# The first heads' values of each pass laid between the parts of the first cross attention

## The chip, the cores and the metric

One NeuronCore of a Trainium2 chip runs the whole program. The metric is the time of one execution on the device in microseconds (us); the kernel before took 2357.95 us, the median of 3 runs (2356.15 to 2360.07). Engines: TensorE (PE, matrix products), VectorE (DVE), ScalarE (ACT), GpSimd (POOL), and SyncE (SP), which here only issues DMAs.

## What is computed

Two layers on x and ctx, both 8 batches of 256 rows of 512, all in float32. The first is a small attention without softmax, with 1x1 convolutions over the 256 rows; the second has two multi-head cross attentions (16 heads of 128) with the same ctx, and an MLP.

```
g_x = conv(g_w, g_b, ctx)^T ; theta_x = conv(theta_w, theta_b, x)^T ; phi_x = conv(phi_w, phi_b, ctx)
W = theta_x @ phi_x / 512 ; y = (W @ g_x)^T
x = batch_norm(conv(w_w, w_b, y)) + x
for l in (1, 2):
    h = layer_norm(x) * scale_l + offset_l
    q, k, v = h @ wq_l + bq_l, ctx @ wk_l + bk_l, ctx @ wv_l + bv_l
    k, v = (k, v with one bias row more, for each head)
    x = x + (softmax(q @ k^T / sqrt(128)) @ v) @ wo_l + bo_l
x = x + gelu((layer_norm(x) * scale + offset) @ w_fc1 + b_fc1) @ w_fc2 + b_fc2
```

## The kernel before

**Precision.** A product of two float32 matrices is made of three fp32r products: each operand is split into a high part (rounded) and a low part (the rest), and `product` (lines 781 to 783) adds high x high, high x low and low x high. So whatever PE multiplies has first been split: weights by POOL, the context and the results by ACT (high) and DVE (low).

**The front part.** Keys and values of both cross attentions depend on ctx alone and are made first and stored in HBM (`kd`, `vd`). The 2048 rows of ctx are taken in two passes of 1024 (`PAIRS`). A pass has eight rounds (`GROUPS`), so rounds r = 0 to 15; a round makes the keys and values of four heads for the pass's 1024 rows. Keys are made by a scheme of seven products in place of eight (`K`, r, i, k: head pair i = 0, 1; P1, P6, P2, P7, P5, P3, P4), from sums of blocks of the weights (`sums`, `keys` on POOL, lines 601 to 640) and sums of blocks of the turned context (T1 to T4, made in `blocks`). Such a group of seven takes 42 instructions on PE. Values are plain: eight row tiles (`V`, r, t) of 12 instructions. A round is K(r, 0), K(r, 1), then V(r, 0) to V(r, 7). A finished key block (`C`) or value tile is staged by ACT and DVE in one of four slots of `stage` and sent by SP.

**The opening.** Ahead of rounds 0 and 8 stands `opening(p)` (line 109): the first cross attention for the four batches b of the pass, in the parts `pg` (two products of ctx with phi and g weights), `M` (their product, 128x128), `th` (theta), `WM`, and `wy` (twice; then ACT makes `aff`, DVE adds x to it, which counts `z_x`, 16 in all, 8 for a pass). Its results pass through PSUM banks S, T and O; ACT copies M, th and WM (`msb`, `th`, `wm`), and DVE adds the bias of pg. Between these parts stand the transposes of the context for the key scheme (`B`, p, i, blk: four blocks for each i), through the four banks of U. In pass 0 ACT and DVE also make the high and low parts of the plain context from the same banks (lines 1036, 1272); the sums T1 to T4 go to a buffer `temp(i, form)`, ACT makes their high part (1044) and POOL the low one (`forms_lo`, 589).

**What sets the order.** Nothing is scheduled: each engine walks the same list `FRONT`, written by `front_order()` and `opening(p)`, in order, and does its part of every item. Only POOL has an order of its own (lines 717 to 745). Semaphores name the counts that an item waits for. PE's wait for an item's weights is on `k_form` (seven for a group of keys) or `split_v` (one for each half of a round's value weights).

```
for r in range(ROUNDS):
    if r % GROUPS == 0:
        for i in range(2):
            forms_lo(r // GROUPS, i)
        sums(r, 1)
        values(r, 0)
        values(r, 1)
        keys(r, 1)
    else:
        values(r, 0)
        keys(r, 1)
        values(r, 1)
    value_bias(r)
```

Behind this, for every round, come `sums(r + 1, 0)` and `keys(r + 1, 0)`, and `sums(r + 1, 1)` where r + 1 isn't the first round of a pass. `keys(r, i)` is seven casts and seven subtractions into `wks`, each cast waiting until PE has used the former form of the same number.

**Buffers.** Many lie over each other. Raw value weights of rounds 0 and 8 (`early_v`) lay over `stage`, as did both early buffers of key sums (`early_s`); later rounds use `rawv` and `ks`, over `pg` and `xb` of the first cross attention. `temp` lay in `z` and in the region `spare`, over `tmp`, `vb` and `raw_vb`.

Of the kernel before, what the change touches and what calls it, by code (L numbers as in the profile page):

```python
# [37 lines left out]
P = 128  # L38
# [70 lines left out]
def opening(p):  # L109

    def blocks(i):
        return [("B", p, i, blk) for blk in range(4)]

    b = 4 * p
    out = [("pg", b, 0), ("pg", b, 1)] + blocks(0)
    for b in range(4 * p, 4 * p + 4):
        more = b + 1 < 4 * p + 4
        out += [("M", b, 0)] + ([("pg", b + 1, 0)] if more else [])
        out += [("th", b, 0), ("WM", b, 0)] + ([("pg", b + 1, 1)] if more else [])
        out += blocks(1) if b == 4 * p else []  # L120
        out += [("wy", b, 0), ("wy", b, 1)]
    return out


def front_order():

    out = []
    for r in range(ROUNDS):
# [112 lines left out]
def bass_xattn(nc, x_in, ctx_in, thw, thb, pgw, pgb, www, bncol, wa, wk, wv, wb, hcol, vrow,  # L241
               lncol, f1col, orow, out):
    ctx = ExitStack()
    with ctx:
# [32 lines left out]
        (wks,) = at(r, 16384, ("wks", [2, 7, 2, P], F32R))  # L277
        wqs, wos = at(r, 16384, ("wqs", [2, CH, 256], F32R), ("wos", [2, 2, D], F32R))
# [6 lines left out]
        early_v = at(r, 8192, ("early_v0", [CH, 256], F32), ("early_v1", [CH, 256], F32))  # L285
        early_s = at(r + 8256, 8256, ("early_s0", [4, 2, P], F32)) + at(r + 3 * 4128, 4128, ("early_s1", [4, 2, P], F32))
# [12 lines left out]
        z = sb("z", [4, D])  # L299
# [4 lines left out]
        (ts,) = at(r, 10240, ("ts", [4, 512], F32))  # L304
# [85 lines left out]
        def temp(i, form):  # L390
            return z[:, form, :] if i == 0 else ts[:, form, :]
# [23 lines left out]
        def _(sp):  # L415
# [17 lines left out]
            def load_value_weights(r):  # L433

                e = r % GROUPS
                for i in range(2):
                    if r:
                        sp.wait_ge(split_v[i], r)
                    if r == GROUPS:
                        for k in range(4):  # L440
                            sp.wait_ge(sent[k], 16 * len(KV) // 8)
# [5 lines left out]
                if e == 0:  # L447
                    sp.wait_ge(t_lo, 8 * (r // GROUPS + 1))
# [3 lines left out]
            def load_x(b):  # L452

                if b == 5:
                    sp.wait_ge(k_form, 7 * (quad(GROUPS, 0) + 1))
# [32 lines left out]
            load_x(0)  # L488
            load_key_weights(0, 0)
            load_x(1)  # L490
            load_key_weights(0, 1)
            bias_row(0)
            load_x(2)
            load_chunk(2)
            load_value_weights(0)
            load_chunk(3)
            load_x(3)

            for what, *a in FRONT:
                if what == "C":  # L500
# [5 lines left out]
                    if (i, o) == (0, C11):  # L506
                        if r + 1 < ROUNDS:
# [8 lines left out]
                elif what == "V":  # L516
# [6 lines left out]
                    if t == 1 and (r + 1) % GROUPS:  # L523
# [3 lines left out]
                    if r == GROUPS - 1 and t == PAIR_TILES - 1:  # L527
                        load_value_weights(GROUPS)
                        load_x(6)
                        load_x(7)  # L530
                    if t == 2 and r + 1 == ROUNDS:
# [5 lines left out]
                        load_values(0)  # L537
            for i in range(4):
# [29 lines left out]
        def _(pool):  # L568
# [975 lines left out]
```

## Time and profile before

| | before |
|---|---|
| median of 3 runs | 2357.95 us |
| the profiled execution | 2355.32 us, its span 2353.5 us |
| PE busy | 2308.7 us (98%) |
| DVE, ACT, POOL busy | 1488.8, 1177.4, 892.9 us |
| chain that ended last | PE 87%, ACT 5%, DVE 3%, POOL 2%, issue 2% |
| granted PE clock, whole span | 0.997 |
| first opening, keys of round 0, values of round 0 | 9.12 to 60.2, to 79.3, to 101.1 us |
| second opening | 390.5 to 430 us |

The span is the time from the first to the last instruction. Matmul records overlap, since the array is pipelined: in a dense stretch a 128x512 fp32r product starts every 0.227 us though its record is 0.39 us long. For the length of a step, starts are to be compared, not durations. The granted clock is a share of 2.4 GHz.

### The profile page before, as it was taken

The page shows a single profiled execution, that of the slowest core. Times are in us where ns is not written, and L with a number is a line of the kernel's source. Part 1 is how long each engine was busy: PE and PEld are TensorE (multiplying, and loading weights), DVE is VectorE, ACT ScalarE, POOL GpSimd, SP SyncE. Part 2 cuts the span into 40 slices and gives each one's busy share as a digit, 9 for nine tenths or more (in the row PEclk, how much of TensorE's full clock was granted, in tenths as well). Part 3 has the DMA queues.
Part 4 walks back from the last instruction along what each step waited for, and adds up shares of the span by engine and source line. Part 5 has one row for each costly group of instructions (what it writes and reads, how often), then busy time and mean ns, then how long its engine had stood idle before and what let it go on. Part 6 is the DMA issues. An engine that isn't in the chain of part 4 may idle for free.

```text
span 2353.5 us, 33519 instructions
## 1 busy us (share of the span) xinstructions
PE 2308.7 (98%) x12144; PEld 1961.7 (83%) x12144; DVE 1488.8 (63%) x2444; ACT 1177.4 (50%) x2897; POOL 892.9 (38%) x876
## 2 busy tenths in 40 slices
PE   7999999999999999999999999999999998999999
PEld 4888888788887788888888878888888887788887
DVE  4777767777777666666666776666666666534433
ACT  3322224322323866666666677666666667322222
POOL 5787876688786430011100253211101114611110
PEclk9999999999999999999999999999999999999999
DMA  4677775577777433333334323343334330100001
GB/s 169 233 269 271 266 278 198 197 251 280 268 267 252 159 121 134 131 126 123 138 121 141 126 85 124 133 141 125 117 126 143 128 134 29 34 30 27 28 1 72
DMA packets 147937, 352.88 MB, mean 150 GB/s; under 512 B 9536, under 2 KB 75584, under 8 KB 131392
## 3 DMA queue, kind: packets, MB, share of 16 engines
q1 hardware_dynamic: 147056, 350.65, 42.9%
q8 instruction: 99, 1.62, 0.3%
q14 instruction: 62, 0.51, 0.1%
q10 hardware_dynamic: 720, 0.10, 0.0%
HBM read 211.78 MB, written 138.94 MB: 149 GB/s over the span
## 4 chain that ended last, share of the span: by engine, by line
PE 87%; ACT 5%; DVE 3%; issue 2%; POOL 2%; DMA 0%; SPq 0%; DVEq 0%; ACTq 0%; POOLq 0%
PE U L781 22%; PE U L783 22%; PE U L782 22%; PE T L909 4%; PE O L781 2%; PE O L783 2%; PE S L783 2%; PE O L782 2%; PE S L781 2%; PE S L782 2%; ACT probs L1125 1%; ACT aff L1084 1%; POOL z L705 1%; ACT probs L1117 1%; DVE hT L1358 1%
## 5 line engine op out<-in xcount | busy, mean ns | idle before, releaser
L580 POOL CAST wos<-raw 128x1024 fp32r<-128x1024 f32 x20 | 20.9, 1047 | 852.9 <-PE U L783 852.9
L1377 DVE TENSOR_TENSOR x<-x,U 128x512 f32<-128x512 f32 x384 | 261.2, 683 | 80.8 <-PE U L783 78.6
L1385 DVE TENSOR_REDUCE nm<-S 128x2 f32<-128x514 f32 x256 | 177.3, 693 | 123.4 <-PE S L783 119.6
L1117 ACT ACTIVATE probs<-S,nm 128x257 f32<-128x257 f32 x512 | 237.7, 476 | 27.2 <-DVE nm L1385 27.2
L1135 ACT ACTIVATE PT<-T 128x512 fp32r<-128x512 f32 x256 | 152.5, 596 | 173.3 <-PE T L909 172.8
L1125 ACT ACTIVATE probs<-probs,rs 128x256 f32<-128x256 f32 x512 | 230.1, 500 | 0.5 <-DVE rs L1389 0.5
L1400 DVE SCALAR_TENSOR_TENSOR oT<-O,hc,oT 128x256 fp32r<-128x256 f32 x256 | 123.8, 484 | 143.1 <-ACT oT L1144 143.1
L781 PE MATMUL U<-wos,oT 128*128 128x512 f32 x512 | 213.4, 417 | 0.3 <-DVE gT L1368 0.2
L1072 ACT ACTIVATE stage<-tmp 128x512 fp32r<-128x512 f32 x128 | 81.1, 633 | 243.9 <-DVE tmp L1350 235.5
L783 PE MATMUL U<-wos,oT 128*128 128x512 f32 x512 | 202.0, 395 | 0.0
L1393 DVE TENSOR_TENSOR PT<-T,PT 128x512 fp32r<-128x512 f32 x256 | 175.5, 686 | 41.8 <-ACT PT L1135 41.8
L782 PE MATMUL U<-wos,oT 128*128 128x512 f32 x512 | 201.3, 393 | 0.0
L781 PE MATMUL U<-wvs,plain 128*128 128x512 f32 x512 | 201.0, 393 | 0.0
L783 PE MATMUL U<-wvs,plain 128*128 128x512 f32 x512 | 200.0, 391 | 0.0
L782 PE MATMUL U<-wvs,plain 128*128 128x512 f32 x512 | 199.9, 390 | 0.0
L1144 ACT ACTIVATE oT<-O,hc 128x256 fp32r<-128x256 f32 x256 | 121.2, 473 | 126.3 <-PE O L783 126.3
L1066 ACT ACTIVATE stage<-z 128x512 fp32r<-128x512 f32 x128 | 81.0, 633 | 196.2 <-DVE z L1311 195.7
L1353 DVE TENSOR_TENSOR stage<-tmp,stage 128x512 fp32r<-128x512 f32 x128 | 107.3, 839 | 102.1 <-ACT stage L1072 102.1
L1103 ACT ACTIVATE tmp<-U,f1c 128x512 f32<-128x512 f32 x64 | 44.0, 688 | 246.1 <-PE U L783 246.0
L909 PE MATMUL T<-ident,probs 128*128 128x128 f32 x1024 | 155.2, 274 | 11.4 <-ACT probs L1125 11.0
L1368 DVE TENSOR_TENSOR gT<-tmp,gT 128x512 fp32r<-128x512 f32 x64 | 57.1, 893 | 165.7 <-ACT gT L1111 165.7
L781 PE MATMUL U<-hT,wqs 128*128 128x512 f32 x384 | 155.7, 405 | 2.4 <-DVE hT L1358 2.4
(196 smaller groups left out, 6717.2 us busy)
## 6 DMA issues: line engine op xcount, KB each, us to landing
kd<-stage SPq DMA_DIRECT2D x128, 516.0 KB, 3.7
kb<-kd SPq DMA_DIRECT2D x64, 1032.0 KB, 4.8
vd<-stage SPq DMA_DIRECT2D x128, 512.0 KB, 5.2
vb<-vd SPq DMA_DIRECT2D x64, 1024.0 KB, 5.0
raw<-wk SPq DMA_DIRECT2D x32, 512.0 KB, 4.9
rawv<-wv SPq DMA_DIRECT2D x28, 512.0 KB, 6.2
raw<-wa SPq DMA_DIRECT2D x24, 512.0 KB, 5.9
raw<-wb SPq DMA_DIRECT2D x24, 512.0 KB, 5.9
```

The costliest lines, as they stand in the source:

```text
L781: pe.matmul(o, lhs[0], rhs[0], start=start, stop=False)
L782: pe.matmul(o, lhs[0], rhs[1], start=False, stop=False)
L783: return pe.matmul(o, lhs[1], rhs[0], start=False, stop=stop)
L909: mm = pe.transpose(T[:, at_:at_ + P], probs[:, J % 2, qt, tt * P:tt * P + P], ident[:])
L1117: ins = act.activation(probs[:, r, qt, 0:257], S[:, qt, 0:257], ACT.Exp, bias=nm[:, r, qt:qt + 1], scale=-1.0, accum_out=sums[:, r, qt:qt ...
L1125: ins = act.activation(probs[:, r, qt, 0:256], probs[:, r, qt, 0:256], ACT.Copy, scale=rs[:, r, qt:qt + 1])
L1135: act.activation(PT[:, J % 2, 0, :], T[:], ACT.Copy).then_inc(pt_hi, 1)
L1144: act.activation(oT[:, 0, h, b * 256:b * 256 + 256], O[:, 0:256], ACT.Identity, bias=hc[:, 3, at_:at_ + 1]).then_inc(o_hi, 1)
L1377: dve.tensor_tensor(x[:, tile, :], x[:, tile, :], bank(what, s, t), ALU.add).then_inc(free, 1)
L1385: dve.tensor_reduce(nm[:, J % 2, :], S[:, :, 0:257], AX.X, ALU.min).then_inc(least, 1)
L1393: dve.tensor_tensor(PT[:, J % 2, 1, :], T[:], f(PT[:, J % 2, 0, :]), ALU.subtract).then_inc(pt, 1)
L1400: dve.scalar_tensor_tensor(out=oT[:, 1, h, to], in0=O[:, 0:256], scalar=hc[:, 3, at_:at_ + 1], in1=f(oT[:, 0, h, to]), op0=ALU.add, op1=AL ...
```

## The change

The values of rounds 0 and 8 are taken out of their rounds and laid into the opening: three tiles with batch b + 1, three with b + 2, two with b + 3. The transposes of i = 1 go ahead of `th` of the first batch. So the value weights and their bias must be split first: POOL now begins a pass with `values(r, 0)`, `values(r, 1)`, `value_bias(r)`, then the low forms, and only then the sums and keys of both head pairs, one after the other. The keys of round 8 are no longer prepared in round 7. The early value weights and the one early buffer of key sums lie over `z`; the sums of (r, 1) for r = 0 and 8 use `ks` and wait until the opening's last add (`z_x`). The temporaries of the context sums lie over `wks`. SP's loads follow: value weights right after the first x, key weights later, x of batches 2, 3, 6 and 7 behind `wy`, value weights of round r + 1 = 1 and 9 with the first keys.

```
 def opening(p):
-    b = 4 * p
-    out = [("pg", b, 0), ("pg", b, 1)] + blocks(0)
-    for b in range(4 * p, 4 * p + 4):
-        more = b + 1 < 4 * p + 4
+    values = [("V", p * GROUPS, t) for t in range(PAIR_TILES)]
+    first = 4 * p
+    out = [("pg", first, 0), ("pg", first, 1)] + blocks(0)
+    for b in range(first, first + 4):
+        more = b + 1 < first + 4
+        early = b == first
         out += [("M", b, 0)] + ([("pg", b + 1, 0)] if more else [])
+        out += blocks(1) if early else [values.pop(0)]
         out += [("th", b, 0), ("WM", b, 0)] + ([("pg", b + 1, 1)] if more else [])
-        out += blocks(1) if b == 4 * p else []
+        out += [] if early else [values.pop(0)]
         out += [("wy", b, 0), ("wy", b, 1)]
+        out += [] if early or not more else [values.pop(0)]
...
-        for t in range(PAIR_TILES):
+        for t in range(PAIR_TILES if r % GROUPS else 0):
...
+        temps = at(r, 16384, ("temp0", [4, 512], F32), ("temp1", [4, 512], F32))
...
+        _, r = region("normalised", 8192)
+        (z,) = at(r, 8192, ("z", [4, D], F32))
+        early_v = at(r, 8192, ("early_v0", [CH, 256], F32), ("early_v1", [CH, 256], F32))
+        (early_s,) = at(r, 4096, ("early_s", [4, 2, P], F32))
...
             load_x(0)
+            load_value_weights(0)
+            load_x(1)
             load_key_weights(0, 0)
-            load_x(1)
             load_key_weights(0, 1)
+            load_chunk(2)
+            load_chunk(3)
             bias_row(0)
-            load_x(2)
-            load_chunk(2)
-            load_value_weights(0)
-            load_chunk(3)
-            load_x(3)
...
                     if (i, o) == (0, C11):
+                        if r % GROUPS == 0:
+                            load_value_weights(r + 1)
...
+                elif what == "wy" and a[1] == 1 and a[0] % 4 < 2:
+                    load_x(a[0] + 2)
...
             def key_sums(r, i):
-                early = r == 0 or (r, i) == (GROUPS, 1)
-                return [(early_s[i] if early else ks)[:, k] for k in range(4)]
+                return [(ks if i or r % GROUPS else early_s)[:, k] for k in range(4)]
...
-                if r == 1 and i == 0:
-                    pool.wait_ge(z_x, TILES // 2)
-                elif (r, i) == (GROUPS, 1):
-                    pool.wait_ge(sent[3], 16 * len(KV) // 8)
-                elif (r, i) == (GROUPS + 1, 0):
-                    pool.wait_ge(z_x, TILES)
+                if r % GROUPS == 0 and i == 0:
+                    pool.wait_ge(split_v[1], r + 1)
+                elif r % GROUPS == 0:
+                    pool.wait_ge(z_x, TILES // 2 * (r // GROUPS + 1))
...
-            sums(0, 0)
-            keys(0, 0)
             for r in range(ROUNDS):
                 if r % GROUPS == 0:
+                    values(r, 0)
+                    values(r, 1)
+                    value_bias(r)
                     for i in range(2):
                         forms_lo(r // GROUPS, i)
+                    sums(r, 0)
+                    keys(r, 0)
                     sums(r, 1)
-                    values(r, 0)
-                    values(r, 1)
                     keys(r, 1)
                 else:
                     values(r, 0)
                     keys(r, 1)
                     values(r, 1)
-                value_bias(r)
-                if r + 1 < ROUNDS:
+                    value_bias(r)
+                if (r + 1) % GROUPS:
                     sums(r + 1, 0)
                     keys(r + 1, 0)
-                if r + 1 < ROUNDS and (r + 1) % GROUPS:
                     sums(r + 1, 1)
```

**PE, first opening.** Before, from the first `pg` on (`T<-pg` is M; `wpg` rows are pg, `wth` th, `www_s` WM, `th,wm` wy, `ident` the transposes):

```order
L951 MATMUL S<-wpg,x 128x256 x8
L813 MATMUL U<-ident,x 128x128 x16
L958 MATMUL T<-pg 128x128 x4
L951 MATMUL O<-wpg,x 128x256 x4
L955 MATMUL S<-xb,wth 128x512 x2
L960 MATMUL S<-www_s,msb 128x256
L951 MATMUL T<-wpg,x 128x256 x4
L813 MATMUL U<-ident,x 128x128 x16
L962 MATMUL O<-th,wm 128x512
L962 MATMUL S<-th,wm 128x512
```

After, up to the first value tile (`wvs,plain_49`):

```order
L812 MATMUL U<-ident,x 128x128 x16
L957 MATMUL T<-pg 128x128 x4
L950 MATMUL O<-wpg,x 128x256 x4
L812 MATMUL U<-ident,x 128x128 x16
L954 MATMUL S<-xb,wth 128x512 x2
L959 MATMUL S<-www_s,msb 128x256
L950 MATMUL T<-wpg,x 128x256 x4
L961 MATMUL O<-th,wm 128x512
L961 MATMUL S<-th,wm 128x512
L957 MATMUL S<-pg 128x128 x4
L950 MATMUL T<-wpg,x 128x256 x4
L780 MATMUL U<-wvs,plain_49 128x512
```

The second set of transposes has moved from in front of the first `wy` to in front of the first `th`, and a value tile follows the third `pg` item.

**POOL, the hand-over from the opening to the key groups of round 0.** Before, after the opening's low forms: the sums of (0, 1) in their own buffer, both splits of value weights, then keys (0, 1):

```order
L589 TENSOR_TENSOR tform_51<-ts,tform_51 128x512 x4
L615 TENSOR_TENSOR early_s_69<-raw 128x256
L616 TENSOR_TENSOR early_s_69<-raw 128x256
L618 TENSOR_TENSOR early_s_69<-early_s_69,raw 128x256
L620 TENSOR_TENSOR early_s_69<-raw,early_s_69 128x256
L648 CAST wvs<-early_v_66 128x4x256
L651 TENSOR_TENSOR wvs<-early_v_66,wvs 128x4x256
L648 CAST wvs<-early_v_67 128x4x256
L651 TENSOR_TENSOR wvs<-early_v_67,wvs 128x4x256
L635 CAST wks<-raw 128x256
```

After, from the last form of keys (1, 0) to the first casts of keys (1, 1), with the sums of (1, 1) and the first split of round 1 between them; ahead of these rows, without anything else, stand sums and keys (0, 1) and sums and keys (1, 0):

```order
L637 TENSOR_TENSOR wks<-raw,wks 128x256
L614 TENSOR_TENSOR ks<-raw 128x256
L615 TENSOR_TENSOR ks<-raw 128x256
L617 TENSOR_TENSOR ks<-ks,raw 128x256
L619 TENSOR_TENSOR ks<-raw,ks 128x256
L647 CAST wvs<-rawv_77 128x4x256
L650 TENSOR_TENSOR wvs<-rawv_77,wvs 128x4x256
L634 CAST wks<-raw 128x256
L634 CAST wks<-ks 128x256
L637 TENSOR_TENSOR wks<-raw,wks 128x256
```

Before, the same rows stand behind round 0's values on PE; now PE has only the key groups (0, 0), (0, 1) and (1, 0) ahead of K(1, 1).

## Rows read from the trace of the kernel before

**Rows 1.** Stretches: us, busy (count) of PE, PEld, DVE, ACT, POOL; PEclk; DMA share; GB/s.
```profile
23.80:27.90 4.10, 4.07 (x12) 3.32 (x13) 0.35 (x2) 0.93 (x2) 4.10 (x5) 0.60 0.00 0
37.20:41.20 4.00, 3.94 (x7) 1.86 (x8) 3.93 (x5) 1.00 (x3) 3.92 (x5) 0.57 0.00 0
...
60.20:79.28 19.08, 19.08 (x86) 15.76 (x84) 16.43 (x28) 6.88 (x18) 15.64 (x24) 1.00 0.46 167
...
390.50:430.00 39.50, 37.12 (x171) 26.49 (x170) 25.50 (x36) 17.10 (x31) 21.06 (x16) 1.00 0.34 107
```

**Rows 2.** Timeline of PE, first opening: start, us, line, operation, [idle before <-releaser].
```profile
9.12 5.83 PE L951 MATMUL S<-wpg,x 128*128 128x256 f32 x16 [9.12 <-DMA pgb_s<-pgb]
14.79 1.91 PE L813 MATMUL U<-ident,x 128*128 128x128 f32 x16
...
17.43 1.89 PE L951 MATMUL O<-wpg,x 128*128 128x256 f32 x8
...
23.83 1.22 PE L960 MATMUL S<-www_s,msb 128*128 128x256 f32 x2 [2.79 <-ACT msb L1008]
...
37.26 3.65 PE L955 MATMUL O<-xb,wth 128*128 128x512 f32 x4 [3.32 <-ACT aff L1019]
...
47.24 1.88 PE L955 MATMUL T<-xb,wth 128*128 128x512 f32 x4
...
51.12 1.02 PE L962 MATMUL S<-th,wm 128*128 128x512 f32 x2
...
55.36 1.95 PE L955 MATMUL S<-xb,wth 128*128 128x512 f32 x4 [1.47 <-issue]
...
58.37 1.12 PE L962 MATMUL T<-th,wm 128*128 128x512 f32 x2 [0.62 <-ACT wm L1010]
```

**Rows 3.** Timeline of DVE: last low part of the first block, last add of the opening.
```profile
22.86 0.68 DVE L1272 TENSOR_TENSOR plain<-U,plain 128x512 fp32r<-128x512 f32 x1
...
61.68 0.68 DVE L1254 TENSOR_TENSOR x<-aff,xb 128x512 f32<-128x512 f32 x1
```

**Rows 4.** Timeline of ACT, first opening.
```profile
23.51 0.26 ACT L1008 ACTIVATE msb<-T 128x128 f32<-128x128 f32 x1
...
28.32 1.09 ACT L1036 ACTIVATE plain<-U 128x512 fp32r<-128x512 f32 x2 [2.86 <-PE U L813]
...
36.35 0.76 ACT L1019 ACTIVATE aff<-O,bns 128x512 f32<-128x512 f32 x1
...
41.53 0.37 ACT L1010 ACTIVATE wm<-S 128x256 f32<-128x256 f32 x1
```

**Rows 5.** Timeline of POOL, first opening: sums, keys, next work, a split of value weights.
```profile
15.01 0.74 POOL L615 TENSOR_TENSOR early_s<-raw 128x256 f32<-128x256 f32 x1 [6.57 <-DMA raw<-wk]
...
17.91 0.40 POOL L635 CAST wks<-raw 128x256 fp32r<-128x256 f32 x1
...
25.13 4.95 POOL L589 TENSOR_TENSOR tform<-z,tform 128x512 fp32r<-128x512 f32 x4
...
47.96 1.04 POOL L648 CAST wvs<-early_v 128x1024 fp32r<-128x1024 f32 x1 [6.42 <-DMA early_v<-wv]
49.07 2.35 POOL L651 TENSOR_TENSOR wvs<-early_v,wvs 128x1024 fp32r<-128x1024 f32 x1
```

**Rows 6.** Timeline of POOL, round 1: keys (1, 1), second split, bias, sums and keys (2, 0).
```profile
105.78 0.40 POOL L635 CAST wks<-raw 128x256 fp32r<-128x256 f32 x1
...
106.48 0.75 POOL L638 TENSOR_TENSOR wks<-raw,wks 128x256 fp32r<-128x256 f32 x1
...
114.47 1.50 POOL L648 CAST wvs<-rawv 128x1024 fp32r<-128x1024 f32 x1
...
118.40 1.74 POOL L658 TENSOR_TENSOR vb<-raw_vb 128x512 f32<-128x512 f32 x1
...
120.11 0.74 POOL L615 TENSOR_TENSOR ks<-raw 128x256 f32<-128x256 f32 x1
...
123.89 0.86 POOL L635 CAST wks<-raw 128x256 fp32r<-128x256 f32 x1
```

More of the change, by code:

```diff
@@ L112, in blocks @@
         return [("B", p, i, blk) for blk in range(4)]
-    b = 4 * p
-    out = [("pg", b, 0), ("pg", b, 1)] + blocks(0)
-    for b in range(4 * p, 4 * p + 4):
-        more = b + 1 < 4 * p + 4
+    values = [("V", p * GROUPS, t) for t in range(PAIR_TILES)]
[4 more added lines that the diff above has]
+        early = b == first
         out += [("M", b, 0)] + ([("pg", b + 1, 0)] if more else [])
+        out += blocks(1) if early else [values.pop(0)]
         out += [("th", b, 0), ("WM", b, 0)] + ([("pg", b + 1, 1)] if more else [])
-        out += blocks(1) if b == 4 * p else []
+        out += [] if early else [values.pop(0)]
         out += [("wy", b, 0), ("wy", b, 1)]
+        out += [] if early or not more else [values.pop(0)]
+    assert not values
     return out
@@ L284, in bass_xattn @@
         (stage,) = at(r, 16512, ("stage", [4, 2, 516], F32R))
-        early_v = at(r, 8192, ("early_v0", [CH, 256], F32), ("early_v1", [CH, 256], F32))
-        early_s = at(r + 8256, 8256, ("early_s0", [4, 2, P], F32)) + at(r + 3 * 4128, 4128, ("early_s1", [4, 2, P], F32))
         (PT,) = at(r, 8256, ("PT", [2, 2, 512], F32R))
@@ L303, in bass_xattn @@
         (wqs_b,) = at(r, 10240, ("wqs_b", [2, CH, 256], F32R))
-        (ts,) = at(r, 10240, ("ts", [4, 512], F32))
         _, r = region("probabilities", 4128)
@@ L390, in temp @@
         def temp(i, form):
-            return z[:, form, :] if i == 0 else ts[:, form, :]
+            return temps[i][:, form, :]
         def middle(i):
@@ L439, in load_value_weights @@
                     if r == GROUPS:
-                        for k in range(4):
-                            sp.wait_ge(sent[k], 16 * len(KV) // 8)
+                        sp.wait_ge(staged, KV["C", GROUPS - 1, 1, C21] + 1)
                     elif e == 1:
@@ L446, in load_value_weights @@
                     sp.wait_ge(vb_ready, r)
-                if e == 0:
-                    sp.wait_ge(t_lo, 8 * (r // GROUPS + 1))
                 sp.dma_start(raw_vb[:].rearrange("p a b n -> p (a b) n"),
@@ L454, in load_x @@
                 if b == 5:
-                    sp.wait_ge(k_form, 7 * (quad(GROUPS, 0) + 1))
+                    sp.wait_ge(k_form, 7 * quad(GROUPS, 0))
                 elif b == 4:
@@ L522, in _ @@
                                  f(value_slots(n)).rearrange("p g q n -> p (g q) n")).then_inc(sent[n % 4], 16)
-                    if t == 1 and (r + 1) % GROUPS:
+                    if t == 1 and r % GROUPS and r + 1 < ROUNDS:
                         load_value_weights(r + 1)
@@ L526, in _ @@
                         load_x(4 if t == 4 else 5)
[L527 to L530, printed above, removed]
                     if t == 2 and r + 1 == ROUNDS:
@@ L819, in keys @@
                 if (r % GROUPS, i, k) == (0, 0, P1):
-                    if p == 0:
-                        pe.wait_ge(formed, formed_before(1, 0))
-                    else:
-                        pe.wait_ge(free, FREE["cT", CHUNKS - 1, CH - 1] + 1)
                     pe.wait_ge(t_lo, 8 * (p + 1))
@@ L841, in values @@
                         pe.wait_ge(split_v[i], r + 1)
+                    if r == 0:
+                        pe.wait_ge(formed, formed_before(1, 0))
+                    elif r == GROUPS:
+                        pe.wait_ge(free, FREE["cT", CHUNKS - 1, CH - 1] + 1)
                 o = take("V", r, t)
@@ L1024, in slot_free @@
                     act.wait_ge(sent[n % 4], 16 * (n // 4))
-                if n % (len(KV) // 2) < 4:
-                    p = n // (len(KV) // 2)
-                    for i in range(2):
-                        act.wait_ge(split_v[i], p * GROUPS + 1)
-                    act.wait_ge(k_form, 7 * (quad(p * GROUPS, n % 4 // 3) + 1))
             def blocks(p, i, blk):
@@ L1315, in products @@
                     if quad(r, i) % (2 * GROUPS) == 0:
-                        dve.wait_ge(t_lo, 8 * (r // GROUPS + 1))
+                        dve.wait_ge(k_form, 7 * (quad(r, i) + 1))
                         dve.wait_ge(z_x, TILES // 2 * (r // GROUPS + 1))
```

1 line of the change is left out of this document (removed).

## Prediction

> **What bounds the kernel now.** I read the page first: TensorE (PE) is busy for 2308.7 of 2353.5 us, so time can be won only where PE waits or runs slowly, and any new wait of PE is paid in full. Then the busy time by stretches, to find those places in the front part. The two openings are the only ones there with waits worth naming. The second takes 39.50 us, of which PE is busy 37.12 [rows 1]. The first runs from 9.12 [rows 2] to 60.2 us, where the stretch of the keys begins: 51.1 us for the same work. The timeline of PE shows why: waits of 2.79, 3.32, 1.47 and 0.62 us, 8.2 in sum [rows 2]. Behind the two longest the granted clock is 0.60 over 4.1 us and 0.57 over 4.0 us, a mixture of the full level (2.4 GHz) and the half one [rows 1]; that costs 4.1 x 0.40 = 1.6 and 4.0 x 0.43 = 1.7 us. So the first opening loses 11.5 us, the second 2.4. Third, the timelines of ScalarE (ACT), VectorE (DVE) and GpSimd (POOL), since the values that now fill the openings are taken away from somewhere: from between the keys of round 0 and those of round 1. Today PE is busy in all of the stretch of round 0's keys, 19.08 of 19.08 us [rows 1], because POOL has made the forms ahead of them, while PE worked on something else.
>
> **What moves.** No PE, DVE or ACT work is added. The 8 value tiles of round 0 (and of round 8) go into the opening, two blocks' transposes come forward, and keys of rounds 0 and 1 (8 and 9) stand back to back: four groups of seven products, where there were two and then 21.8 us of values. A group is half of the stretch 60.20 to 79.28, 9.54 us [rows 1]. Let S be the start of K(0, 0) on PE, and let V mean value tiles.
>
> **First opening, after.** PE ends pg(1, 0) at 17.43 + 1.75 = 19.2. Now the four transposed blocks of i = 1 follow; 16 transposes take 1.9 us [rows 2], so one block 0.45. Each needs a bank that DVE empties only with the low part of the former block, and the last of those ends at 23.5 [rows 3]. PE is therefore through them at 24.0 instead of 21.0: 3.0 us lost. th, WM and pg(1, 1) take 51.12 - 47.24 = 3.9 us [rows 2], up to 27.9. The next item, wy, needs ACT's copies of th and WM, and these now stand behind ACT's copies of the second block. That chain took from 28.32 to 36.35, 8.0 us [rows 4]; it can begin after the copy of M, at 23.8, and ends at 31.8; th (a 128x512 copy like the aff of 0.76) and wm (0.37) take about 1.1 more [rows 4], so wy starts at 32.9. A wait of 5.0 us, and the slow clock once behind it, 1.7. The low clock that follows the wait among the blocks hides under the 5.0 us. New losses 3.0 + 5.0 + 1.7 = 9.7 against 11.5: a gain of 1.8. From there on V tiles lie between the items, 2.7 us each, and cover the shorter waits. The value weights are no obstacle: they take the place in SP's queue of the key weights that had landed by 15.0 [rows 5], two splits of 3.4 us [rows 5] are done by 22, and PE's first V comes near 38. POOL then still has eight low forms, the sums and the first keys (2.9 + 7.2 us), which end near 44, far ahead of S near 80; that cover is wide. SP's x loads wait for wy's adds, near 37 for the first, and the block that needs it comes some 20 us later by the same count. Bounds of this term: -2 (the clock falls twice) and +8.5 (neither the 5.0 nor its slow clock comes).
>
> **Second opening, after.** Its first block has no low parts to make, so banks come free sooner and the chain on ACT is shorter; I take 0.4 us for the new wait, so a gain of 2.4 - 0.4 = 2.0, between 0 and 2.4. The keys of round 8, that POOL used to make during the values of round 7, now come after the low forms, some 25 us before they are used: hidden.
>
> **Start of the keys, after.** This is the term that decides. The sums of the second key group (r, 1) no longer have a buffer of their own. They go to `ks`, which lies over `pg` and `xb`, and POOL waits for z_x = 8, the last add of the opening. That add ended 61.68 + 0.68 = 62.4 [rows 3], 2.2 us behind S at 60.2; the last V ahead of it on DVE adds 0.3, so POOL starts at S + 2.5. Before, these sums were made in the opening. From there POOL has, in its order, before V(1, 0) can run: sums(0,1), keys(0,1), sums(1,0), keys(1,0), sums(1,1), values(1,0), keys(1,1), values(1,1). Nothing in it can be skipped, and there is no stretch of V in which to catch up.
>
> Prices, from the same work beside K products in round 1: keys 8.7 (from 105.78 to 114.47, the first form after 1.4), values 3.9, sums 3.8 us [rows 6]. Prices where DVE has little to do, in the first opening: sums 2.9, keys 7.2, values 3.4 [rows 5]. With the first set:
> keys(1,0): first form ready at S + 2.5 + 3.8 + 8.7 + 3.8 + 1.4 = S + 20.2, PE there at S + 19.1: wait 1.1.
> keys(1,1): first form at S + 2.5 + 2 x (3.8 + 8.7) + 3.8 + 3.9 + 1.4 = S + 36.6; PE there at 20.2 + 9.5 = S + 29.7: **wait 6.9**. Within a group POOL's step of 1.24 us is shorter than PE's 1.36, so only the first form is waited for.
> V(1,0): POOL at S + 35.2 + 8.7 + 3.9 = S + 47.8; PE, with one slow-clock cost, at 36.6 + 9.5 + 1.7 = S + 47.8. Without waits it would be S + 38.2. Loss 9.6 us a pass.
> While PE waits, DVE runs dry, and then sums(1,1) and values(1,0) should go at the opening's prices, and part of the keys too: 0.9 + 0.5, with some 0.2 of keys, 1.6 less. Loss 8.0. I take the middle of the two, 8.8, because the wait is about half as long as the work that it could relieve. Bounds: 1.9 a pass if all goes at the opening's prices (S + 2.5 + 5.8 + 14.4 + 2.9 + 3.4 + 1.5 = S + 30.5 against S + 28.6), 12 if nothing is relieved and DVE, with four groups in a row, falls back far enough to hold banks.
>
> What the trace shows is that the same first cast of a key group takes 0.40 us in the opening [rows 5] and 0.86 at 123.89, while the low parts of the keys are made [rows 6]. The Trainium skill, "GPSIMD Engine Reference", section 1 (Specifications), says that GpSimd's SBUF interface is shared with VectorE and contended by VectorE instructions that have two SBUF inputs. By that rule the low parts of keys and values on DVE are what slows POOL, and they stop when PE waits: the sum would go by 8.0 a pass and end 1.6 us lower.
>
> **Sum.** 2 x 8.8 - 1.8 - 2.0 = +13.8. The profiled execution took 2355.3, so 2369.1 by it; the median of the runs lies 2.6 above that execution, giving 2371.8. I say **2371**. About 0.2% (4.7 us) is what a measurement of this kernel can tell from no change.
>
> **Rivals.**
> 1. POOL is fast enough (5%). All its work goes at the opening's prices: loss 2 x 1.9 = 3.8, gains 3.8, time 2355 to 2358. For it: these are prices that the trace has, for the same operations. Against it: the full key group of round 1, 8.7, where PE and DVE worked as they will here [rows 6].
> 2. Faster (4%). The values fill what they were put into: wy does not wait at all, since ACT's chain of the second block takes less than the 3 us that PE gives it, and the three stalls of the old order are covered. Gains 11.5 + 2.4, loss 3.8 if POOL is fast too: 2355.3 - 10.1 = 2345. It decides where the loss at the keys is below 7 us a pass. Against it: ACT's chain for the second block is 8.0 us long though its transposes lay done on PE within 2 us of its start [rows 2, 4]; it is paced by the turn-taking with DVE, not by PE.
> 3. Worse than forecast (13%). No relief while PE waits, V(1, 0) waits for its second split behind a late keys(1, 1), and DVE lags over 28 products in a row: 12 us a pass, no gain in the first opening, 2355 + 24 - 2 = 2377, in the runs 2380. For it: POOL and DVE slow each other, as the two prices show [rows 5, 6]. Against it: through two groups in a row PE is never held, 19.08 of 19.08 us [rows 1], and DVE rests in the waits.
> 4. The forecast as above (78%): 8 to 9.6 us a pass.
>
> **How the numbers follow.** The forecast and rival 3 are slower, 91%; rival 1 is within 0.2%, 5%; rival 2 faster, 4%. The range leaves out rivals 1 and 2 and holds the forecast with its bounds: low, 6 us a pass and a first opening better by 4, 2355 + 12 - 8 + 3 = 2362; high, rival 3 at 2380.
>
> **What would show it.** Right: in the profile after, PE idle ahead of the first product of K(1, 1), some 29 us behind K(0, 0), for 5 to 7 us, released by POOL's `wks`; the same in round 9; a granted clock below 1 there; POOL without a gap from the last add of the opening to the end of the splits of round 1; PE idle for about 5 us before the first wy, released by ACT's `wm` or `th`; and from the V tiles of round 1 on, everything as before but late by the same amount. The span between K(0, 0) and V(1, 0) near 47 us. Wrong: PE busy through that stretch (then POOL's prices were too high), or PE idle at the first V of the opening released by a load (then SP's order was misread), or waits released by DVE within K products (then rival 3).

## The result and the profile after

The changed kernel took 2376.95 us (median of 4 runs, 2376.11 to 2379.76), beside 2357.71 for the kernel before. The ratio is 1.0089, 95% interval 1.0077 to 1.0101: slower by 19 us. 2371 had been forecast, with 2362 to 2380 as range.

The page of the profile after, its span, its first part and the shares of the chain:

```profile
span 2375.2 us, 33501 instructions
...
PE 2318.0 (98%) x12144; PEld 1968.4 (83%) x12144; DVE 1481.1 (62%) x2444; ACT 1175.2 (49%) x2897; POOL 884.8 (37%) x876
...
PE 59%; ACT 5%; DVE 4%; issue 1%; POOL 1%; DMA 0%; SPq 0%; DVEq 0%; ACTq 0%; POOLq 0%
```

The span grew by 21.7 us and PE's busy time by 9.3, at the same number of products: part of the loss is a slower clock, the rest waiting. The view of waits, PE's own:

```profile
PE U L780 <- POOL wks L637: 17.0, 4, 6.1
PE T L908 <- ACT probs L1119: 11.0, 15, 2.9
...
PE O L961 <- ACT wm L1009: 3.3, 2, 3.0
...
PE U L812 <- DVE plain L1266: 2.5, 3, 1.3
```

The first line is new: four waits for key forms, 17.0 us. The kernel before had none. The third and fourth are the two new waits of the openings.

**First opening.** Timeline of PE (start, us, then what ended the idle time before):

```profile
20.05 0.66 PE L812 MATMUL U<-ident,x 128*128 128x128 f32 x4 [0.72 <-DVE plain L1266]
21.25 0.66 PE L812 MATMUL U<-ident,x 128*128 128x128 f32 x4 [0.54 <-DVE plain L1266]
23.18 1.11 PE L812 MATMUL U<-ident,x 128*128 128x128 f32 x4 [1.27 <-DVE plain L1266]
24.09 3.00 PE L954 MATMUL S<-xb,wth 128*128 128x512 f32 x4
...
32.26 1.22 PE L961 MATMUL O<-th,wm 128*128 128x512 f32 x2 [3.01 <-ACT wm L1009]
```

The banks' waits, 2.5 us, and the wait for ACT's copy are where the prediction put them [rows 2, 4]. PE came there later, since `th` ran at the low clock (3.00 us, not 1.88), so 3.0 us were left to wait, not 5.0, and wy started at 32.3, with 32.9 forecast. Opening and eight tiles took from 9.03 to 78.9, 69.9 us; before, opening and tiles took 51.1 + 21.8 = 72.9. Gain 3.0, with 1.8 forecast.

**Second opening.** One wait of 0.26 us is left of 2.4:

```profile
412.98 1.12 PE L961 MATMUL O<-th,wm 128*128 128x512 f32 x2 [0.26 <-ACT wm L1009]
```

It starts at 399.1 and ends at 458.0; 58.9 against 39.5 + 21.8 = 61.3. Gain 2.4, with 2.0 forecast.

**The keys.** Stretches from the first product of K(0, 0) on, columns as in [rows 1]:

```profile
78.90:98.00 19.10, 19.10 (x85) 15.58 (x83) 17.10 (x28) 6.35 (x16) 13.81 (x21) 1.00 0.64 222
98.00:101.50 3.50, 0.18 (x1) 0.00 (x0) 2.13 (x3) 1.12 (x4) 3.42 (x6) 0.99 1.06 374
101.50:112.90 11.40, 11.35 (x42) 8.95 (x42) 6.31 (x9) 3.08 (x9) 11.10 (x17) 0.85 0.57 198
112.90:116.50 3.60, 0.00 (x0) 0.00 (x0) 3.60 (x3) 0.31 (x1) 3.60 (x5) 0.80 0.57 189
116.50:128.00 11.50, 11.46 (x39) 9.26 (x40) 5.75 (x8) 2.04 (x6) 11.42 (x14) 0.76 0.35 135
```

The first stretch holds two key groups, in 19.1 us as in [rows 1]. Then PE waits 3.4 us for K(1, 0), which takes 11.4 us in place of 9.5 at a granted clock of 0.85, and waits 3.7 us for K(1, 1). That group takes 12.2 us, from 116.54 to the first product of V(1, 0); the last row ends a little before it, with 0.76. The clock thus falls twice a pass, each time behind a wait:

```profile
101.53 0.79 PE L780 MATMUL U<-plain,wks 128*128 128x512 f32 x1 [3.35 <-POOL wks L637]
...
116.54 0.80 PE L780 MATMUL U<-plain,wks 128*128 128x512 f32 x1 [3.65 <-POOL wks L637]
...
128.71 0.39 PE L780 MATMUL U<-wvs,plain 128*128 128x512 f32 x1
```

V(1, 0) starts 49.8 us behind K(0, 0); 38.2 would be without waits: a loss of 11.6 us, with 8.8 forecast. In the second pass K(8, 0) starts at 458.0 and V(9, 0) at 511.55, 53.6 us: a loss of 15.4. Together 27.0, less 5.4 of gains: 21.6 of the 21.7 us.

POOL's side, where it rested in this stretch (timelines of POOL, first and second pass):

```profile
81.65 0.74 POOL L614 TENSOR_TENSOR ks<-raw 128x256 f32<-128x256 f32 x1 [36.84 <-DVE x L1248]
...
96.24 0.74 POOL L614 TENSOR_TENSOR ks<-raw 128x256 f32<-128x256 f32 x1 [2.46 <-DMA raw<-wk]
...
126.70 1.75 POOL L657 TENSOR_TENSOR vb<-raw_vb 128x512 f32<-128x512 f32 x1
...
460.71 0.74 POOL L614 TENSOR_TENSOR ks<-raw 128x256 f32<-128x256 f32 x1 [30.81 <-DVE x L1248]
...
475.80 0.74 POOL L614 TENSOR_TENSOR ks<-raw 128x256 f32<-128x256 f32 x1 [2.96 <-DMA raw<-wk]
```

S is again the start of K(0, 0), here 78.9. POOL starts at S + 2.75, behind the last add, as forecast (2.5). From there to the end of the splits it takes 45.0 us, and rests once: 2.46 us; in the second pass it rests 2.96, for the raw key weights of (1, 0) or (9, 0). The timeline of the second pass has also this, between sums(9, 1) and values(9, 0):

```profile
490.40 4.40 POOL L691 TENSOR_TENSOR rstd<-vpe,minus_half 128x4 f32<-128x4 f32 x4
494.76 1.24 POOL L647 CAST wvs<-rawv 128x1024 fp32r<-128x1024 f32 x1
```

Those are four power operations (`deviation`) that POOL does once at the end of round 8. The timeline of SP shows why the raw weights were late:

```profile
86.57 1.43 SPq L450 DMA_DIRECT2D rawv<-wv  x2
88.04 0.46 SPq L453 DMA_DIRECT2D raw_vb<-vrow  x1
88.56 0.42 SPq L438 DMA_DIRECT2D raw<-wk  x1
```

They are issued behind three loads of 512 KB, at 88.56, and land 7.6 us later.

### The profile page after: what moved, and what is told of

Same layout as the page of the kernel before. It is cut to its first block, busy times and chain, and to the rows that moved or that the text cites. A ratio compares the mean times of both kernels' runs of the same rounds, so it can differ in the third digit from the quotient of the medians.

```text
span 2375.2 us, 33501 instructions
## 1 busy us (share of the span) xinstructions
PE 2318.0 (98%) x12144; PEld 1968.4 (83%) x12144; DVE 1481.1 (62%) x2444; ACT 1175.2 (49%) x2897; POOL 884.8 (37%) x876
## 4 chain that ended last, share of the span: by engine, by line
PE 59%; ACT 5%; DVE 4%; issue 1%; POOL 1%; DMA 0%; SPq 0%; DVEq 0%; ACTq 0%; POOLq 0%
PE U L780 14%; PE U L782 13%; PE U L781 13%; PE T L908 4%; PE S L782 2%; PE O L780 2%; PE S L781 2%; PE O L782 2%; PE S L780 2%; PE O L781 2%; ACT aff L1078 1%; DVE hT L1352 1%; ACT probs L1119 1%; ACT probs L1111 1%; ACT hT L1081 1%
## 5 line engine op out<-in xcount | busy, mean ns | idle before, releaser
L1347 DVE TENSOR_TENSOR stage<-tmp,stage 128x512 fp32r<-128x512 f32 x128 | 102.5, 801 | 105.9 <-ACT stage L1066 105.9
L908 PE MATMUL T<-ident,probs 128*128 128x128 f32 x1024 | 155.1, 274 | 11.3 <-ACT probs L1119 11.0
```

Source lines behind the costliest of these rows:

```text
L908: mm = pe.transpose(T[:, at_:at_ + P], probs[:, J % 2, qt, tt * P:tt * P + P], ident[:])
```

## The experiments

The theory now: POOL's chain sets when PE can begin K(1, 1) and K(9, 1), and so when V(1, 0) and V(9, 0) start; the chain is its own work plus a load and, in the second pass, the power operations. Eleven kernels. Times are medians of 5 to 11 runs; each was measured with runs of the kernel before beside it (2356.5 to 2357.9, so about 1 us between two medians says little).

### The load and the power operations, one at a time

```
                     if (i, o) == (0, C11):
-                        if r % GROUPS == 0:
-                            load_value_weights(r + 1)
                         if r + 1 < ROUNDS:
                             load_key_weights(r + 1, 0)
...
+                        if r % GROUPS == 0:
+                            load_value_weights(r + 1)
```

> Edit: behind the first key block of rounds 0 and 8 the key weights of the next round are loaded ahead of its value weights, not behind them. Theory (POOL's chain from the last add of the opening to the splits of round 1 sets the start of V(1, 0), and the late load of raw weights lengthens it): POOL's waits for raw of 2.46 and 2.96 us ahead of sums(1, 0) and sums(9, 0) go, the chain is that much shorter, V(1, 0) and V(9, 0) start 2.5 and 3.0 us earlier: 5.4 us less than the changed kernel, about 2371.5. Rival 1 (the wait only moves, to the split of the value weights, which now land later): 0 to 1 us less. Rival 2 (PE's own slow clock behind its waits is the bound, not POOL): only the first wait shrinks and V starts about 1 us earlier, 2 us in sum.

Measured 2372.92 us, 4.0 less than the changed kernel. In POOL's timeline the rest of 2.46 us is gone, with 0.49 of another kind left:

```profile
93.77 0.74 POOL L614 TENSOR_TENSOR ks<-raw 128x256 f32<-128x256 f32 x1 [0.49 <-POOL wks L637]
```

That is 2.0 us less rest in the first pass where 2.5 were expected, and K(1, 1) starts 1.2 us earlier behind K(0, 0), K(9, 1) 2.0 us: POOL's own work from there to the start of keys(1, 1) now takes longer, 19.6 us in place of 18.4, with a shorter pause of PE beside it (1.4 us, not 3.4). The theory holds, somewhat smaller; both rivals expected less than what came.

```
-                if r == GROUPS:
+                if r == GROUPS + 1:
                     for c in range(CHUNKS):
                         deviation(0, c)
```

> Edit: POOL's four small power operations (rstd) of round 8 are done behind round 9. Theory: they stand between sums(9, 1) and values(9, 0), 4.4 us on POOL's chain in the second pass, so PE's wait ahead of K(9, 1) of 6.1 us falls to about 1.7 and the time by 4.4 us or a little more if the slow clock behind it goes too: 2372.5. Rival (PE waits for the value split behind keys(9, 1) instead): less than 2 us gained.

Measured 2372.68 us, 4.3 less. But the wait ahead of K(9, 1) fell to 3.3 us, not to 1.7, and from K(8, 0) to V(9, 0) only 2.9 us were won, because POOL now rested longer for the raw weights of (9, 0):

```profile
476.11 0.72 POOL L614 TENSOR_TENSOR ks<-raw 128x256 f32<-128x256 f32 x1 [4.47 <-DMA raw<-wk]
```

The rest lies in the first opening (0.9 us shorter in this execution) and in the first pass (0.8), where this edit changes nothing. So the run alone doesn't price the operations. In the old order they took 4.0 us beside values on PE (460.09 to 464.09), and POOL rested 7.6 us behind them: there they cost nothing.

The run with both edits and all eight tiles, told further down, does price them. From the timelines of PE, in us behind the first product of K(0, 0) or K(8, 0):

| | median | K(1, 1) | V(1, 0) | K(9, 1) | V(9, 0) |
|---|---|---|---|---|---|
| changed kernel | 2376.95 | 37.6 | 49.8 | 41.9 | 53.6 |
| key weights first | 2372.92 | 36.4 | 47.5 | 39.9 | 51.9 |
| power operations later | 2372.68 | 37.7 | 49.0 | 39.5 | 50.7 |
| both | 2369.71 | 36.4 | 48.7 | 36.0 | 47.3 |

With the weights in time, the power operations are worth 3.9 us at K(9, 1) and 4.6 at V(9, 0). The first pass of the second and the last row runs the same instructions, and V(1, 0) differs by 1.2 us, since K(1, 1) took 11.0 us in one and 12.3 in the other behind the same wait of 5.79 us: the slow clock behind a wait is not the same each time. The start of K(1, 1) is the steadier measure.

### The missing buffer of key sums

```
+        (late_s,) = at(r + 6144, 4096, ("late_s", [4, 2, P], F32))
...
-                return [(ks if i or r % GROUPS else early_s)[:, k] for k in range(4)]
+                return [(ks if r % GROUPS else late_s if i else early_s)[:, k] for k in range(4)]
...
                 elif r % GROUPS == 0:
-                    pool.wait_ge(z_x, TILES // 2 * (r // GROUPS + 1))
+                    pool.wait_ge(vb_ready, r + 1)
```

> Edit: the sums of (0, 1) and (8, 1) get a buffer of their own again (over the raw bias rows, whose next load goes behind the second key group), so POOL makes them in the opening and keys(0, 1) starts with the first product of K(0, 0). Theory of the prediction (the missing buffer is what makes POOL late): the chain begins some 5 us earlier, the loss at the keys falls by 4 us a pass, 2369. Rival (the next thing in the chain, raw weights of (1, 0), lands no earlier than about S + 16, since its load is issued at the first staged key block and behind two value weights): POOL waits there instead, and only the 1.3 us of the moved bias load is won: 1 to 3 us in sum, 2374 to 2376. I hold the rival for likelier.

Measured 2377.27 us, not to be told from the changed kernel (2376.95). POOL began the keys of (0, 1) 1.6 us behind the start of K(0, 0), as soon as PE had used the first form, and not 5.6; then it waited:

```profile
97.73 0.74 POOL L627 TENSOR_TENSOR ks<-raw 128x256 f32<-128x256 f32 x1 [4.18 <-DMA raw<-wk]
```

What it won ahead of the load it lost in front of it: the rival was right. Its 1 to 3 us are there in the profile, 0.1 us from K(0, 0) to V(1, 0) and 2.2 from K(8, 0) to V(9, 0), but not in the time: the profiled execution had also a first opening longer by 2.3 us, of which the last section tells. The five runs go from 2374.7 to 2379.0.

To price the buffer without that load in the way, the next two have the key weights of (1, 0) and (9, 0) loaded in the opening, and the power operations later; the first has the buffer too:

```
                 elif what == "wy" and a[1] == 1 and a[0] % 4 < 2:
                     load_x(a[0] + 2)
+                    if a[0] % 4 == 1:
+                        load_key_weights(a[0] // 4 * GROUPS + 1, 0)
```

> Edit: all eight tiles stay in the opening; own buffer for the sums of (r, 1), the key weights of (1, 0) and (9, 0) loaded in the opening (behind the second batch's wy), the power operations behind round 9. Theory (POOL's chain is the bound, and it is now only late by its own work): keys(0,1) end near S + 12, keys(1,0) are never waited for, keys(1,1) are waited for by 3.5 us with one slow clock, V(1,0) and V(9,0) start near S + 43.4 instead of S + 49.5 and S + 53.6: 16 us less than the changed kernel, 2361; still slower than before, since four groups' forms do not fit. Rival (with its three delays gone the chain fits under PE): V at S + 38.2 to 40, 2350 to 2353.

> Edit: as the last, but without the own buffer for the sums. Theory: both delays go, the loads (2.5 and 3.0 us) and in the second pass the power operations (4.4 us); they lie one behind the other on POOL, so they add: 9 to 10 us less, 2367 to 2368. Against the last run it prices the missing buffer: 3 to 3.5 us a pass, 6.5 in sum. Rival (the buffer is worth nothing even now, since PE's use of the forms paces keys(0,1)): both runs within 2 us of each other.

Measured 2365.70 with the buffer and 2369.68 without it: 4.0 us, not 6.5. By the profiles V(1, 0) and V(9, 0) start 46.2 and 46.2 us behind K(0, 0) and K(8, 0) with it, 47.7 and 48.3 without: 1.6 and 2.1 us, of which 1.5 and 0.9 are waits (5.7 and 5.8 us with it; 1.4, 0.3 and 5.5, and 1.0 and 5.7, without). The profiled execution of the second had again a longer first opening, by 3.0 us, which its median seems not to have: it is the slowest of its five. Part of what the buffer gives ahead is taken back by PE's pace through K(0, 0), since a form can't be made before the old one is used: POOL rests 0.98 us and then 0.26 us time and again, released by PE. And the run with the buffer stays 8 us above the kernel before, with POOL never kept waiting for more than 1.1 us. PE's timeline in it has one wait a pass:

```profile
112.55 0.80 PE L795 MATMUL U<-plain,wks 128*128 128x512 f32 x1 [5.67 <-POOL wks L652]
```

5.7 us where 3.5 were expected. The three sequences ahead of it on POOL took 9.2 (keys), 3.4 (sums) and 4.2 us (a split), by and large the prices of [rows 6] or above: with PE no longer waiting at K(1, 0), DVE had no pause, and POOL worked at its slow rate. Its time missed the forecast of 2361 by 4.7 us: V starts at S + 46.2 where S + 43.4 was expected. So POOL's own work alone does not fit beside four key groups.

### How many tiles the opening may take

```
+PLACES = [(1, 0), (2, 1), (3, 0), (3, 1)]
+EARLY_TILES = len(PLACES)
...
-    values = [("V", p * GROUPS, t) for t in range(PAIR_TILES)]
+    values = [("V", p * GROUPS, t) for t in range(EARLY_TILES)]
...
-        out += blocks(1) if early else [values.pop(0)]
+        out += blocks(1) if early else tile(b - first, 0)
...
-        for t in range(PAIR_TILES if r % GROUPS else 0):
+        for t in range(0 if r % GROUPS else EARLY_TILES, PAIR_TILES):
```

`tile` gives a tile where its place is in the list; the rest follow K(r, 1).

> Edit: four value tiles in each opening (one with batch 1, one with batch 2, two with batch 3), the other four behind K(r, 1) as before the change. Theory (the waits of PE come from four key groups in a row, not from the opening): the 10.9 us of values between K(0, 1) and K(1, 0) give POOL the time it lacks in the first pass, and all but some 2 to 4 us in the second, where the power operations lie on the chain too; all openings' gain of 5 us stays. 2350 to 2355, faster than or equal to the kernel before. Rival (the opening needs all eight tiles to cover its waits): the gain of the opening shrinks to 2 us, 2356 to 2360.

Measured 2357.83 us, ratio to before 1.0006 (0.9997 to 1.0015): 19 us better than the changed kernel, and level with the old one. The first pass had no wait for a form; the second had one, 4.7 us, at K(9, 1), and I had expected 2 to 4. POOL's timeline ahead of it has the power operations, 4.17 us, and a rest of 3.50 us for the raw weights of (9, 0); no run with four tiles takes them apart. With both seen to:

> Edit: four tiles in the opening, four behind K(r, 1); key weights loaded ahead of value weights, power operations behind round 9. Theory: the run with four tiles alone lost 4.7 us of waiting and some 1.8 of slow clock ahead of K(9, 1), because of the power operations; both go, no wait for a key form is left in either pass: 6 us less than that run, 2351 to 2352, faster than the kernel before by 5. Rival (the wait there came from the load of raw weights as well and from the number of groups): 2354 or more.

Measured **2350.44 us** (6 runs, 2349.09 to 2351.67), ratio 0.9970 (0.9958 to 0.9981): faster than the kernel before by some 7 us, and than the change by 26. PE's waits in the front part of it:

```profile
PE S L958 <- DMA pgb_s<-pgb: 9.2, 1, 9.2
PE O L969 <- ACT wm L1017: 3.1, 2, 2.9
PE U L820 <- DVE plain L1274: 2.5, 3, 1.3
```

No wait for a form is left, and V(1, 0) and V(9, 0) start 38.1 us behind K(0, 0) and K(8, 0), the four tiles between them not counted. The same two edits with eight and with six tiles in the opening:

> Edit: the changed kernel, all eight tiles in the opening, with the key weights loaded ahead of the value weights and the power operations behind round 9; the run with four tiles and the same two edits took 2350.4. Theory: the two delays lie one behind the other on POOL and add as they were measured alone (4.1 and 4.3 us less): 2368 to 2369, some 18 us above the run with four tiles, all of it at the keys. Rival (both edits remove the same wait): 2371 to 2372.

> Edit: as the last, but six tiles in the opening and two behind K(r, 1). Theory: each tile behind K(r, 1) gives POOL 2.73 us, so two give 5.5 a pass; with eight in the opening PE waits about 6.5 to 7 us a pass and then once or twice at the slow clock, so 1 to 1.5 us of waiting is left and hardly any slow clock: 2353 to 2356. Rival (the waits are not a matter of POOL's time between the groups, but of loads behind the opening): 2360 or more.

Eight tiles: 2369.71 us, so the two edits nearly add (4.0 + 4.3 = 8.3, and 7.2 came). Six: 2358.77, ratio 1.0006 (0.9998 to 1.0015). So with four, six and eight tiles 2350.4, 2358.8 and 2369.7. Two tiles a pass are 4 x 2.73 = 10.9 us of PE work, and the step from six to eight costs 10.9 us: there POOL's chain sets the end, and PE time laid ahead of the keys buys nothing. From four to six it is 8.3, so, as an estimate from these three times, the limit is between four and five tiles. The 2353 to 2356 expected for six took the waits too small and left out the slow clock: they were 3.0 and 2.5 us, and the group behind each took 11.3 us and not 9.5, 1.7 us more each time:

```profile
110.42 0.50 PE L788 MATMUL U<-plain,wks 128*128 128x512 f32 x1 [3.03 <-POOL wks L645]
...
482.23 0.50 PE L788 MATMUL U<-plain,wks 128*128 128x512 f32 x1 [2.51 <-POOL wks L645]
```

### The place of the second block's transposes

The last with four tiles, and

```
-        out += blocks(1) if early else tile(b - first, 0)
+        out += tile(b - first, 0)
...
-        out += tile(b - first, 1)
+        out += blocks(1) if early else tile(b - first, 1)
```

> Edit: as the last, but the second block's transposes stand where they stood before the change, in front of the first wy. Theory (the new place costs 3.0 us in banks and 3 to 5 us of waiting for ACT's wm, with the slow clock twice, and only the wait of 2.8 us ahead of WM comes back): the first V tile then waits about 2 us for the low parts of the plain context, and the first opening is 1 to 3 us shorter, 2349 to 2351. Rival (the value tile's wait and WM's wait with its slow clock eat it): the same as the last run or up to 2 us more.

Measured 2350.64, the same. PE's timeline has the old wait ahead of WM and a new one at the first tile:

```profile
23.81 1.22 PE L967 MATMUL S<-www_s,msb 128*128 128x256 f32 x2 [2.79 <-ACT msb L1015]
...
36.47 0.47 PE L788 MATMUL U<-wvs,plain 128*128 128x512 f32 x1 [2.70 <-DVE plain L1274]
```

5.5 us of waiting in place of 5.4, and the first opening was 0.5 us longer, not 1 to 3 shorter: as far as the waits show, ACT's and DVE's chain through the blocks costs the same in either place. The rival held.

### What slows POOL beside the keys

```
-                dve.tensor_tensor(key_slot(1, n), by_batch(z[:, o, :]), f(key_slot(0, n)), ALU.subtract)...
+                dve.tensor_tensor(key_slot(1, n), by_batch(z[:, o, :]), by_batch(S[:, 0, :]), ALU.subtract)...
```

> Edit: as the run with eight tiles and both edits, but DVE takes PSUM bank S as second operand of the low part of a key block, in place of the high part in SBUF, so one operand comes from SBUF, not two; the low parts of the keys are then something else than the reference's, the work is the same in count and size. Theory (what slows POOL beside K products is DVE's instructions with two SBUF operands): POOL's key groups fall from 8.1 to 9.2 us to 7.2 to 7.6, sums from 3.3 to 2.9, the chain by 4 to 5 us a pass, and the time by 8 to 10 us against that run. Rival (any DVE work slows it, or the DMAs do): POOL's groups stay above 8 us and the time within 3 us.

Measured 2365.39 us, 4.3 below the run with eight tiles. The groups of POOL and DVE from 80 to 125 us (counts, busy us, mean ns), first of that run with eight tiles:

```profile
L637 POOL TENSOR_TENSOR wks<-ks,wks 128x256 fp32r<-128x256 f32 x12 | 9.2, 769 | 0.0
L637 POOL TENSOR_TENSOR wks<-raw,wks 128x256 fp32r<-128x256 f32 x9 | 8.0, 888 | 0.0
L634 POOL CAST wks<-ks 128x256 fp32r<-128x256 f32 x12 | 6.2, 516 | 0.0
...
L1337 DVE TENSOR_TENSOR stage<-z,stage 128x512 fp32r<-128x512 f32 x13 | 12.4, 951 | 2.0 <-ACT stage L1060 2.0
```

and of the one with the second operand in PSUM:

```profile
L637 POOL TENSOR_TENSOR wks<-ks,wks 128x256 fp32r<-128x256 f32 x12 | 8.9, 741 | 0.0
L637 POOL TENSOR_TENSOR wks<-raw,wks 128x256 fp32r<-128x256 f32 x9 | 6.7, 740 | 0.0
L634 POOL CAST wks<-ks 128x256 fp32r<-128x256 f32 x12 | 4.8, 402 | 0.0
...
L1337 DVE TENSOR_TENSOR stage<-z,S 128x512 fp32r<-128x512 f32 x14 | 9.6, 685 | 2.0 <-ACT stage L1060 2.0
```

POOL's operations fall to one duration, 740 and 402 ns, the opening's (0.74 and 0.40 us), with DVE busy for 30.2 of the 45 us (30.4 in the other), ACT for 13.0 (11.8) and the DMAs for a share of 0.67 (0.63); DVE's own falls from 951 to 685. That the two operands alone are not what makes DVE slow is shown by its adds of aff and xb, both in SBUF, while POOL rests for them (run with eight tiles and both edits, PE and ACT at work):

```profile
80.19 0.68 DVE L1248 TENSOR_TENSOR x<-aff,xb 128x512 f32<-128x512 f32 x1
...
81.04 0.74 POOL L614 TENSOR_TENSOR ks<-raw 128x256 f32<-128x256 f32 x1 [35.87 <-DVE x L1248]
```

So DVE instructions with two operands from SBUF and POOL's work slow each other. K(1, 1) and K(9, 1) started 2.7 and 1.7 us earlier. In the time only half of the 8 to 10 us came, since POOL now overtook the next load:

```profile
104.83 0.74 POOL L614 TENSOR_TENSOR ks<-raw 128x256 f32<-128x256 f32 x1 [2.19 <-DMA raw<-wk]
...
480.73 0.74 POOL L614 TENSOR_TENSOR ks<-raw 128x256 f32<-128x256 f32 x1 [2.54 <-DMA raw<-wk]
```

## Why the prediction was right, and where it was short

**Right in sign, cause and place.** POOL's chain from the opening's last add sets the start of V(1, 0) and V(9, 0), and PE waits at the key groups for `wks`. The tile counts show it most directly. The forecast was +13.8 us, +19.2 came (21.7 between the two profiled executions). The sum of the prediction gives 2371.7 for the median, and 2371 was said; this difference is within the noise.

**The openings** gained 3.0 and 2.4 us, forecast 1.8 and 2.0. The 5.0 us for ACT's wm was 3.0, because the slow clock that I had hidden under the wait took its place; the sum of both was right within 0.6 us.

**The step that failed is "Nothing in it can be skipped"**, the list of POOL's work from S + 2.5 to V(1, 0), with a loss of 8.8 us a pass; 11.6 and 15.4 were measured. The list was complete in operations of keys and values, and left out two things. First, the raw weights of (1, 0): my text on the loads looked at those of the opening and not at the three that the change puts ahead of this one, 2.46 and 2.96 us of rest. Second, the four power operations at the end of round 8: I had not walked through POOL's code behind the sums; 4.4 us on the chain. Taking both away won 7.2 us of time. What is left is what had been priced: in that run K(1, 1) and K(9, 1) start at S + 36.4 and S + 36.0, where the prediction had 36.6 without relief and 35.8 with half of it. Its loss is still 19.6 us, not 17.6: 0.8 from these starts, and 1.2 since the two groups took 12.3 and 11.3 us, where 9.5 + 1.7 had been summed.

**That the time fell into the range is partly luck.** Its high end, 2380, stood for another cause, rival 3; nothing in the range was kept for a late load or for other work on POOL's chain.

**The place of the first wait.** I had 1.1 us ahead of K(1, 0) and 6.9 ahead of K(1, 1); the trace has 3.4 and 3.7 in the first pass. The load moved the first; keys(1, 0) took 8.4 us (from 99.6 to 107.95) and not 8.7. The clock fell behind both waits, where I had it fall once. The first fall, 1.9 us over K(1, 0), was hidden, since PE had to wait for K(1, 1) behind it anyway. The second, 2.6 us over K(1, 1), was not: V(1, 0) was never waited for, and POOL had its second split ready at 126.7, 2.0 us ahead.

**The relief.** The reckoning that POOL works at the opening's prices while PE waits, half of which I took, is borne out in part: sums(1, 1) and values(1, 0) took from 107.95 to 114.60, 6.7 us with the gap before them, where the beside-key prices give 7.7 and the opening's 6.3. Sums(0, 1) too took 2.9 us, the opening's price, though PE did not wait there. What the Trainium skill states in "GPSIMD Engine Reference", section 1 (Specifications), on VectorE instructions with two SBUF inputs agrees with the last experiment: 740 ns with one such input, up to 888 with two. The prices in [rows 5, 6] had shown POOL's side of it only; that POOL slows DVE too came out in that experiment.

**The rivals.** POOL as fast as in the opening (1) is excluded by every run with eight tiles. The faster case (2) would have needed a loss at the keys below 3 us a pass. Rival 3 gave a time nearer to the one that came, 2380 against 2376.95, than the forecast did, but by another way: DVE never held a bank within the keys in the view of waits, and the openings did gain.

## What to carry to other kernels

When filler work is moved into a hole, look at what it covered where it stood: here 21.8 us of values gave POOL its time for the next forms, and POOL, a helper busy for 37% of the span, was the bound of a 50 us stretch. Walk the helper's whole program through the stretch that lost its cover, loads and odd jobs included, and sum it. The share to move is then the one at which both sides are just covered: four of eight tiles with two delays taken off the chain beat both kernels.

## What was not expected of the hardware

When the clock falls behind a chain of small waits is not the same in every execution, with the same instructions ahead of it. In the first opening of eleven profiles PE goes through the same three waits (0.72, 0.54 and 1.27 us). In nine of them `th` right behind runs slowly, 2.9 to 3.5 us for 1.9, as in the changed kernel:

```profile
24.09 3.00 PE L954 MATMUL S<-xb,wth 128*128 128x512 f32 x4
...
41.13 1.88 PE L954 MATMUL O<-xb,wth 128*128 128x512 f32 x4
```

In the other two (c_own_sums and g_prefetch_pow; here the second) it runs at full speed, PE comes early to the wait for wm, waits 4.6 us in place of 3.0, and the low clock comes behind that, where nothing hides it (0.50 over 4.7 us; 0.63 over 3.8 us behind the shorter wait of the changed kernel):

```profile
24.70 1.88 PE L956 MATMUL S<-xb,wth 128*128 128x512 f32 x4
...
33.29 2.08 PE L963 MATMUL O<-th,wm 128*128 128x512 f32 x2 [4.55 <-ACT wm L1011]
...
43.23 1.88 PE L956 MATMUL O<-xb,wth 128*128 128x512 f32 x4
```

From the first product, at 9.03 and 8.82 us, to the second `th` it is 32.1 us in the first and 34.4 in the second; in the whole set 31.0 to 34.4. Part of this comes earlier, for a reason that the profiles don't show: the opening's first 16 products of pg took 5.2 to 6.5 us in the nine and 6.7 in the two. From the first wy to the second `th` it is 7.2 us in four of the nine, 8.9 in the other five and 9.9 in the two. So here the slow clock was free where it fell ahead of a wait that was there anyway, and cost up to 2.7 us where it fell behind; runs that differ by less than that should be compared stretch by stretch. Why the clock fell where it did stays open, and so does whether the two kernels do so in each execution, as only one of each was profiled.
